# A two-layer transformer kernel: the expert stage's first loads and input split issued during layer 1's last steps

## What is computed

```python
h = _layernorm(x) * (1 + ca) + sa
x = x + ga * L0_attn(h)          # 16 heads, rms norm, rotary
h = _layernorm(x) * (1 + cb) + sb
x = x + gb * L0_ffn(h)           # ternary weights
h = _layernorm(x) * (1 + ca) + sa
x = x + ga * L1_attn(h)          # each head divided by its mean norm, then gate and Wo
h = _layernorm(x) * (1 + cb) + sb
x = x + gb * L1_ffn(h)           # layernorm @ attn_w + h, 8 experts, next_w, gelu
```

## Time and profile before

| | us |
|---|---|
| median of 3 runs | 1984.94 (1984.57 to 1988.12) |
| the profiled execution's own time | 1994.66 |
| its span | 1993.0 |
| its mean granted clock | 0.954 |
| the expert stage in that span (its first instruction to the end) | 1690.27 to 1993.0 |
| PE, DVE, ACT, POOL busy | 91%, 67%, 58%, 33% |

### The profile page before, as it was taken

One profiled execution on the slowest core, in us unless ns is written; L12 is line 12 of the kernel. 1 busy time (PEld: TensorE's weight loads), 2 busy tenths in 40 slices (PEclk: granted clock), 3 DMA queues, 4 the chain that ended last, 5 costly groups with the idle time before them and its releaser, 6 DMA issues. The chain is left out here.

```text
span 1993.0 us, 29496 instructions
## 1 busy us (share of the span) xinstructions
PE 1820.3 (91%) x10344; PEld 754.6 (38%) x10344; DVE 1345.1 (67%) x2598; ACT 1150.1 (58%) x1553; POOL 654.5 (33%) x918
## 2 busy tenths in 40 slices
PE   4789999999979999999999997899999997499998
PEld 3323333332224444444444443223233322355554
DVE  5488889888744535535535542688888884689993
ACT  4368778876743333424334232478778776477774
POOL 5667687761220000000000112234444311335452
PEclk8689999999989999999999998699999999699999
DMA  3345545444262000000001004333332320624410
GB/s 118 64 93 123 136 120 123 107 108 99 86 219 98 22 11 12 22 1 22 22 1 48 11 11 75 53 75 71 68 67 59 65 38 29 232 79 144 158 44 32
DMA packets 119620, 147.65 MB, mean 74 GB/s; under 512 B 19779, under 2 KB 102838, under 8 KB 117430
## 3 DMA queue, kind: packets, MB, share of 16 engines
q1 hardware_dynamic: 119478, 145.79, 27.7%
HBM read 100.34 MB, written 45.14 MB: 73 GB/s over the span
## 5 line engine op out<-in xcount | busy, mean ns | idle before, releaser
L853 DVE TENSOR_REDUCE A_M<-A_SM 128x1 f16<-128x512 f32 x1024 | 654.4, 683 | 137.8 <-PE A_SM L1068 135.2
L624 ACT ACTIVATE A_P<-A_ST 128x1024 f32<-128x1024 f32 x512 | 523.6, 1025 | 166.1 <-PE A_ST L1084 161.8
L1068 PE MATMUL A_SM<-A_KT,A_QS 48*128 48x512 f16 x1024 | 354.9, 399 | 45.2 <-DVE A_M L853 37.5
L1619 PE MATMUL B_PA<-B_Hh,B_wh 128*128 128x512 f16 x1024 | 388.1, 379 | 3.1 <-DVE B_Hl L1584 3.1
L1619 PE MATMUL B_PA<-B_Hl,B_wh 128*128 128x512 f16 x1024 | 388.1, 379 | 0.0
L1538 ACT ACTIVATE B_af<-B_PA,B_sv 128x512 f32<-128x512 f32 x192 | 131.9, 687 | 357.2 <-PE B_PA L1619 357.0
L1084 PE MATMUL A_ST<-A_QS,A_KT 49*128 49x512 f16 x1024 | 300.3, 386 | 2.6 <-DMA A_QS<-A_rows 2.1
L1101 PE MATMUL A_AV<-A_P,A_V 128*32 128x512 f32 x2048 | 275.2, 609 | 4.2 <-ACT A_P L624 3.6
L1582 DVE TENSOR_SCALAR B_Hh<-B_af 128x512 f16<-128x512 f32 x128 | 62.8, 490 | 278.8 <-ACT B_af L1538 278.8
L1068 PEld LDWEIGHTS A_SM<-A_KT,A_QS 48*128 48x128 f16 x1024 | 83.3, 93 | 432.7 <-DVE A_M L853 382.1
L1333 POOL TENSOR_TENSOR B_hl<-B_hf,B_hh 128x512 f16<-128x512 f32 x14 | 16.2, 1156 | 506.4 <-ACT B_hh L1349 506.4
(11 more groups left out here) (362 smaller groups left out, 3246.1 us busy)
## 6 DMA issues: line engine op xcount, KB each, us to landing
D_w_st<-in_we_dram SPq DMA_DIRECT2D x16, 1024.0 KB, 7.2
qk<-A_tr SPq DMA_DIRECT2D x58, 256.0 KB, 2.5
A_KT<-qk SPq DMA_DIRECT2D x96, 128.0 KB, 5.0
A_QS<-qk SPq DMA_DIRECT2D x96, 128.0 KB, 4.9
A_w_st<-in_w_ffn_dram SPq DMA_DIRECT2D x32, 352.0 KB, 3.4
A_QS<-A_rows SPq DMA_DIRECT2D x512, 0.5 KB
w_hi<-A_f_hi SPq DMA_DIRECT2D x32, 176.0 KB, 3.4
w_lo<-A_f_lo SPq DMA_DIRECT2D x32, 176.0 KB, 3.9
```

Source lines behind the costliest of these rows:

```text
L624: nc.scalar.activation(P[:, st, 2 * pair:2 * pair + 2, :], ST[:, u % 2, :, :], ACT.Exp, scale=1.0 / math.sqrt(HD)).then_inc(exp_s, 1)
L853: nc.vector.tensor_reduce(M[G % 2][:, o:o + 1], SM[:, n % 2, :], AX, ALU.max, negate=True).then_inc(max_s, 1)
L1068: nc.tensor.matmul(SM[:, n % 2, :], QS[b % 2][r, 2 * g + pair, tt * 128:tt * 128 + 128], KT[b % 2][r, 2 * g + pair, :], start=True, stop=T ...
L1619: ins = nc.tensor.matmul(out, a, c, start=start and kt == 0 and n_ == 0, stop=stop and kt == kts[-1] and n_ == len(ops) - 1)
```

## The change

Everything is in layer 1's attention, `experts`, and the few lines that call them. In `attention`, three things are added to layer 1's list of steps:

```diff
+LAST_AT = dict(LOADS=244, SPLIT0=250, SPLIT1=251)
@@ block.sync
             for p in range(BEGIN, END):
                 step(p)
+                if not L0 and p == LAST_AT["LOADS"]:
+                    sp.wait_ge(xn_s, TT * B)
+                    keep["experts"]["sync"](sp)
@@ block.gpsimd
+                    if not L0 and p == LAST_AT[f"SPLIT{f}"]:
+                        keep["experts"]["gpsimd"](pool, f)
@@ block.scalar
                 step(p)
+                if not L0 and p == PAIRS * B:
+                    nc.scalar.preload_act_table_set("sqrt_and_others")
```

`experts` becomes a generator, entered before layer 1's attention runs. Up to its first yield it takes tiles at the right end of SBUF and semaphores that live longer (prefix E_, cleared with a barrier at the very end), and defines what layer 1 calls. The 20 loads, and their order, are those of before:

```diff
+        def first_loads(sp):
+            load_w, load_tokens, load_x, load_rows = loads_of(sp, [yT0], [by_token(keep["rare"])], [rows0])
+            sp.dma_start(gates...); sp.dma_start(hsel...); sp.dma_start(gcol...)
+            load_x(0)
+            sp.dma_start(wsm...); bo; rowf; vec
+            load_tokens(0)
+            load_rows(0)
+            load_w(0, 0)
+            load_w(0, 1)
+            sp.dma_start(eb...)
+        def split_input(pool, f):
+            pool.wait_ge(y_ld[0], 64)
+            y_ = yT0[:, f, :, :].rearrange("p a t -> p (a t)")
+            nc.gpsimd.tensor_copy(yh[:, f, :], y_).then_inc(y_high, 1)
+            pool.wait_ge(y_high, f + 1)
+            nc.gpsimd.tensor_tensor(yl[:, f, :], y_, yh[:, f, :], ALU.subtract).then_inc(y_low, 1)
+        yield {"sync": first_loads, "gpsimd": split_input}
```

(The diff above gives the DMA starts in short form.) In the stage itself rsc goes into the projection's weights and no longer into the input, with gates scaled by WS / H instead of 1 / H:

```diff
+                act.wait_ge(nsel, 4)
+                act.wait_ge(c_ld[4], 16)
+                for f in range(FT):
+                    nc.scalar.activation(wsh[:, 0, f, :], wsm[:, 0, f, :], ACT.Copy, scale=rsc[:, f:f + 1])
...
-                    v = yT[e % 2][:, f, :, :]
-                    nc.scalar.activation(v, v, ACT.Copy, scale=rsc[:, f:f + 1]).then_inc(y_sc, 1)
```

In body 0 alone, the work of a = 0 comes first on each engine: TensorE gate(0) ahead of project(1); DVE D_gf ahead of the weights of expert 1; ScalarE D_gh ahead of them and of the split of input 2; GpSimd D_gl ahead of the tokens of input 1. In the other bodies the order is that of before:

```diff
             def body(b, e, a, m):
+                if a is not None and m is None:
+                    gate(a)
...
-                    if a is not None and c == 1:
+                    if a is not None and m is not None and c == 1:
                         gate(a)
```

More of the change, by code:

```diff
@@ L1727, in experts @@
[L1727 to L1743, removed]
@@ L1754, in experts @@
[L1754 to L1761, removed]
@@ L1774, in experts @@
[L1774 to L1779, removed]
+        right = lambda n, s, t=F32: ctx.enter_context(nc.sbuf_tensor("D_" + n, s, t, side="right"))
+        gates, hsel, gcol = right("gates", [128, H]), right("hsel", [128, FT, H]), right("gcol", [H, 1])
@@ new lines, in experts @@
+        bo, rowf = right("bo", [H, C]), right("rowf", [2, 2, C])
+        wsm, vec, eb = right("wsm", [128, 3, FT, C]), right("vec", [128, 3, FT]), right("eb", [128, E8, HM + FT])
+        w_st = right("w_st", [128, 2, FT * HID])
+        yT0, rows0 = right("yT0", [128, FT, 2, EH]), right("rows0", [128, 2, NROWS, C])
+        yh, yl = right("yh", [128, FT, T], F16), right("yl", [128, FT, T], F16)
+        c_ld = [lasting(f"c_ld{k}") for k in range(8)]
+        w_ld, y_ld, x_ld = ([lasting(f"{n}_ld{k}") for k in range(2)] for n in "wyx")
@@ L1781, in halves, with loads_of @@
+        r_ld = [lasting(f"r_ld{k}") for k in range(3)]
+        y_high, y_low = lasting("y_high"), lasting("y_low")
         def halves(e):
             return e // 2, e // 2 + 4, slice((e % 2) * EH, (e % 2) * EH + EH)
[L1785 to L1791, removed]
+        def loads_of(sp, yT, x2t, rows, x3_s=None, x4_s=None, e_low=None):
@@ new lines, in experts @@
+        sem = phase_semaphores(nc, ctx, "D_")
+        nsum, rinv = sb("nsum", [128, H]), sb("rinv", [128, H])
+        selw = sb("selw", [128, 2, FT, H])
+        rsc, gsc = sb("rsc", [128, FT]), sb("gsc", [128, FT])
+        ones = sb("ones", [128, 128])
+        gcol2 = sb("gcol2", [H, 2])
+        wsh, wsl = sb("wsh", [128, 3, FT, C], F16), sb("wsl", [128, 3, FT, C], F16)
+        bT = sb("bT", [128, FT])
+        rowh, row2 = sb("rowh", [2, 2, C], F16), sb("row2", [128, 2, C], F16)
+        second_row, vec_ws = sb("second_row", [2, 1]), sb("vec_ws", [128, FT])
@@ L2101, in _ @@
             nc.vector.tensor_scalar(vec_ws[:, :], vec[:, 0, :], WS, None, ALU.mult).then_inc(vec_s, 1)
+            dve.wait_ge(nsel, 4)
+            for f in range(FT):
+                dve.wait_ge(cw_high, f + 1)
+                nc.vector.scalar_tensor_tensor(out=wsl[:, 0, f, :], in0=wsm[:, 0, f, :], scalar=rsc[:, f:f + 1],
+                                               in1=wsh[:, 0, f, :], op0=ALU.mult, op1=ALU.subtract).then_inc(cw_low, 1)
             def constants():
@@ L2229, in _ @@
             pe.wait_ge(ones_s, 5)
-            pe.wait_ge(nred, 1)
-            nc.tensor.matmul(X[:, 0, 0:H], ones[:, :], nsum[:, :], start=True, stop=True).then_inc(ntot, 1)
             pe.wait_ge(gcol_s, 1)
@@ L2241, in _ @@
             ins.then_inc(bT_mm, 1)
-            pe.wait_ge(cw_low, 1)
+            pe.wait_ge(nred, 1)
+            nc.tensor.matmul(X[:, 0, 0:H], ones[:, :], nsum[:, :], start=True, stop=True).then_inc(ntot, 1)
+            pe.wait_ge(cw_low, FT)
             pe.wait_ge(row_low, 1)
```

161 lines of the change are left out of this document (89 added, 72 removed).

## The result

The changed kernel takes 2005.37 us (median of 8 runs, 1994.9 to 2011.02), the kernel before 1986.63 beside it (8 runs, 1983.48 to 1993.25): a ratio of 1.0084, 95% interval 1.0058 to 1.0109. The ratio is that of the two means, 2004.18 and 1987.55; the medians are 18.7 us apart. On the 1984.94 of before it is +16.7 us (+11.5 to +21.6), or 2001.6. The forecast was +13.8 and 1998.7, with 1990 to 2003.5 as its range; the median of 2005.37 itself lies above that range. The kernel before, run beside it, took 1.7 us more than the 1984.94 that the range starts from; the difference of the medians, put on 1984.94, gives 2003.7, the upper edge. The profiled execution after took 2005.03, its span is 2003.3.

What follows compares the result with a forecast made beforehand. The prediction saw the removable wait in the expert stage's opening, where bo lies behind wsm. Its terms 16.3 + 2.0 - 6.2 + 1.2 + 0.5 gave +13.8 us on 1984.94, 1998.7 us; own range 1995 to 2003, with rivals 1990 to 2003.5.

Steps and rivals of the forecast that it cites:

- the store is not late for ScalarE: Rival at the wait before batch 7's first half, step 249: no stall or cold start, -4.5 us, 1980.4; chance 0.07.
- The stall, +16.3: Layer 1's tail: batch 6's store, 21st issue behind the loads, lands late; ScalarE stands still, +16.3 us.
- my upper bound of 17.5: ScalarE's wait for batch 6's store: 5.1 MB of loads plus the store's 0.5 at 261 GB/s, at most +17.5 us.
- The rival by issue time alone: Batch 6's store only waits for its turn to be issued: delay 8.0 us, sum +5.5, 1990.4; chance 0.09.
- The stopped TensorE, +2.0: Layer 1's tail: TensorE stops some 15 us without exponentials and restarts at half clock, +2.0 us, bounds 0 to +3.
- The opening, -6.2: Start of the expert stage: with constants loaded, projection 0 starts at +7.3 to +7.5, not +13.6: -6.2 us, bounds -7.2 to -5.0.
- its bad bound: Opening of the expert stage: row2 in the way of wsl at its length of before, gain only -5.0 us.
- The rival that folding and preloading do less than they say: Opening of the expert stage held by something else: only 3 us gained there, 2001.9; chance 0.06.
- Body 0, +1.2: Expert 0's body, gate(0) first: first product starts 2 to 4 us earlier but TensorE waits for input 1, +1.2 us.
- the bad end of the range: Body 0, gate(0) first: another cold start in the new idle of some 3 us, up to +3.5 us.
- The end, +0.5: End of the kernel: one more clearing of semaphores with its barrier, +0.5 us, bounds 0 to +1.4.

Runs made afterwards that it cites:

- experiment 1: The changed kernel with its 20 loads at step 246, behind batch 6's store of y, instead of step 244: 1984.88 us, ratio 0.9985.
- experiment 3: The changed kernel with loads still at step 244, but batch 7's y written into another tile, so ScalarE needn't wait for batch 6's store: 1986.23 us, ratio 0.9987.
- experiment 4: The changed kernel with only expert 0's two weight loads (2.1 MB) at step 244 ahead of the store, the other 18 at step 246: 1991.92 us.
- experiment 5: The changed kernel with 11 small loads (0.6 MB) at step 244 ahead of the store, the 9 large ones at step 246: 2000.47 us.
- experiment 8: The changed kernel with loads at 246, body 0's old order, the program's own semaphores and no preloaded square root table: 1984.67 us, ratio 0.9974 to the kernel before.
- experiment 7: The changed kernel with loads at 246, body 0's old order and the program's own semaphores (one clearing and barrier less): 1984.09 us, ratio 0.9979 to the kernel before.
- experiment 2: The changed kernel with loads at step 246 and body 0 in its old order on all four engines: 1982.95 us, ratio 0.9970 to the kernel before.

## Why the prediction was right, and where it was off

**The mechanism and the sign.** "The store becomes the 21st issue", ScalarE "makes it wait there for the landing of that store": experiments 1 and 3 remove one each, the order and the tie, and each alone removes the whole idle. The rival "the store is not late for ScalarE" falls with the first row of the profile after.

**The stall, +16.3, measured +17.7.** The sum was right in its parts and short in two. From the first load's issue to the store's landing I had 20.2 us; it was 21.6. The 20 issues took 9.44 instead of 9.07, and the landing behind the store's issue 12.2 instead of 11.1. My "1.0 to 1.5 us" for the 384 KB more was too little by about 1. The idle came out just over my upper bound of 17.5; the prediction's range allowed "+1.5" for it, where that bound is only +1.2. That bound took 261 GB/s from the first issue on. The stretch from 1672.40 to 1690.00 moved 295 GB/s, 5.2 MB of the 5.6, so the 4.2 us ahead of it moved only some 0.4 MB: what was missing is the slow beginning.

**The rival by issue time alone.** It gave 8 us of delay. Experiment 4 has almost no issue time in front of the store and 5.84 us of idle, so the queue of bytes counts. My estimate for one megabyte ahead that has not moved when the store is issued is 2.6 to 3.0 us, from 2.1 to 3.3 MB (experiments 3 and 4 and the changed kernel). The Trainium skill, "DMA: Bandwidth & Descriptors", section "Queues, rings and completion order", has each ring consumed in order and the semaphore's increment ordered behind the earlier writes of that engine. By that the store's semaphore could not come before the loads ahead of it had moved, and the runs with large loads agree: 2.8, 8.8 and 12.2 us with 0, 2.1 and 3.1 MB left to move. The prediction took the same section to let the store overtake; its words are on a later transfer that runs on one DMA engine and an earlier one that runs on sixteen, and no run here shows a store overtaking.

**The stopped TensorE, +2.0, measured +1.2.** The step that failed is that the value matmuls "become the longest item when doubled": only the first 8 took 1.93, the next 1.25, and from 1698.08 on they took 1.07. I had let the tail run cold to its end. The restart itself is best read up to ScalarE's copy into A_ysb: from the move of batch 7's first half it is 8.09 us in the changed kernels without a stall, 9.37 after the stall of 17.7 us, 9.70 in experiment 4 and 10.22 in experiment 5. So a restart costs 1.3 to 2.1 us, and not more after the longer stop. With the 0.13 of the preload that is +1.4 in the kernel after; the other 0.2 us of the difference to +1.2 were won back behind it, where TensorE's last turns ran at full speed. The term's bounds, 0 to +3, held.

**The opening, -6.2, measured -6.4.** In detail too: +7.26 to projection 0 where +7.3 to +7.5 was forecast, and the chain ran through bT's product, the sum over partitions, rinv and rsc as written. Behind rsc it went on through the split rows (L2129, 0.68 us) and then both wsl, 0.88; the prediction had the rows in the way only as its bad bound, and the two wsh, which it counted, lay beside them. Against the three profiles with the old opening (13.63, 13.24 and 13.08) the gain is 5.8 to 6.4. The rival that folding and preloading do less than they say falls; that the table saves nothing in the opening is shown by experiment 8.

**Body 0, +1.2, measured +1.6.** D_x of input 1, D_x(1), was to end between 1738.1 and 1739.6 with D_h2l at 1729.0; D_h2l ended 7.6 us later after (1736.6), and D_x at 1747.2, which is 1739.6. D_xn(1) ended at 1762.55, forecast 1754.9 + 7.6 at the latest. So the chain stood at its late edge, and the idle with its cold turn, which I had as the bad end of the range, is the rule: D_xn(0) to D_xn(1) takes 29.13 to 29.52 us in six profiles with the gate first and 26.27 to 27.03 in six with the old order, 2.6 us more on the mean. The +1.6 of the table is less because projection 0 to D_xn(0) took 0.7 us less that time (21.79 and 21.09; the two profiles of the kernel before have 21.79 and 20.36). The term was mis-sized by 1.4; its sign held.

**The end, +0.5, measured +0.3**, by the kernel after and experiment 7. The +0.4 in the table's last row is no measure of it, since that row holds the steady part too.

**On balance** the short stall and the long cold start cancelled in part: +13.8 forecast, +14.6 by the stretches, +16.7 (11.5 to 21.6) by the runs. What is left between the last two is inside the interval. The mechanism is shown; that the sum came so near is in part luck, since the stall's +1.4 and the cold start's -0.8 have opposite signs.

**What beats both.** The opening's gain is real and was buried under the stall. Experiment 2, with the loads behind the store and the old order of body 0, is 0.30% faster than before (0.11 to 0.48). By its stretches the opening gives -6.4, the seam takes +0.5 (14.26 for 13.74) and the end +0.3: -5.6, and 0.30% is 6.0 us (2.2 to 9.5). These stretches leave out the part behind the opening, which is also shorter in that profile, by 0.9 us up to the turn of D_xn(1) and by 3.3 from there to the end; both are inside the spread of single profiles with the old order (46.63 to 48.82 us and 237.03 to 240.51). Experiments 7 and 8 don't differ from it measurably.

## What to carry to other kernels

A load that is moved forward costs what it is moved past: write down every DMA behind it in that queue and who waits for its landing, and count both the issues and the bytes ahead that will not have moved yet. A tile that exists once ties a compute engine to the landing of its store; where the slack is one microsecond, put the store first or give the next user another tile. And when an order is changed so that one product starts earlier, look for the engine's next input: here the idle moved from in front of the product to behind it and grew a cold start.

## What was not expected of the hardware

- Behind many loads the issue itself is held: the store's took 6.92 us in the kernel after and 5.92 in experiment 3, while the other engines went on where nothing tied them to it. The count of issues alone does not decide it: in experiment 1 the 21st issue is the small eb, and it took 0.57 us (1672.99 to 1673.56) with as much in front of it.
- TensorE came back to full speed within some 5 us in layer 1's tail, although it was partly idle there (8 matmuls in 1.93, 1.25, then 1.07 us). In body 0 it stood idle for 4.16 us, and the granted clock over the next 7.7 us was 0.63. In experiment 2 it stood idle for 5.22 us in front of the first product, and the turn of D_ht(1), 8.17 us after that product's start, took 1.04 for 8.
- The steady part has two periods, 31.17 and 31.67 us an expert, in the same kernel and even in one run. What selects them is open.
- The seam of the changed kernels is some 0.1 to 0.8 us longer without any stall: 13.86 to 14.33 us in six profiles, 13.54 to 13.79 in the three with the old opening. Besides the preload's 0.13 us it is what comes behind the copy into A_ysb. Where TensorE still runs both of its last turns at full speed (0.66 and 0.63 us for 4 matmuls, granted clock 0.96 and more over the seam), the seam is 13.54 us with the old opening and 13.86 with the new one; where they take 0.72 to 1.10 and 1.08 or 1.09 us (clock 0.81 to 0.83), it is 13.74 and 13.79, and 14.05 to 14.33. The barrier at the end of layer 1 (the idle of GpSimd in front of the expert stage) takes 1.29 to 1.42 us with the old opening, and 1.43 to 1.84 in the changed kernels without a stall, where 5 MB of loads move in the seam. Whether the loads are the cause, and what selects the clock there, wasn't tried.
